# A float32 transformer layer on one core: the low half of the output weights made in three operations with a signal each

## What is computed

```
x = x + cross_attention(layernorm(x), ctx)     # 512 context tokens of width 384 for each batch
h = layernorm(x)
q, k, v = h @ wq, h @ wk, h @ wv               # self-attention within a batch of 64 tokens
q, k = rope(q), rope(k)
p = softmax(where(causal, q @ k.T / sqrt(32), -inf))
x = x + (p @ v) @ wo                           # wo: 512 x 512
h = layernorm(x)
top, idx = top_k(h @ w_router, 32)             # half of the tokens of each batch
y = gelu(h[idx] @ W1 + b1) @ W2 + b2           # 512 -> 2048 -> 512
x = x + (h with sigmoid(top) * y added at idx)
```

## Time and profile before

| what | value |
| --- | --- |
| median of 3 runs | 1198.59 us (1198.58 to 1198.82) |
| the profiled execution | 1198.52 us |
| its span, first to last instruction | 1196.7 us |
| PE busy | 1182.8 us, 99% of the span |
| DVE busy | 747.8 us, 62% |
| ACT busy | 624.0 us, 52% |
| POOL busy | 600.0 us, 50% |
| granted TensorE clock | 1.000 |

### The profile page before, as it was taken

One profiled execution on the slowest core, in us unless ns is written; L12 is line 12 of the kernel. 1 busy time (PEld: TensorE's weight loads), 2 busy tenths in 40 slices (PEclk: granted clock), 3 DMA queues, 4 the chain that ended last, 5 costly groups with the idle time before them and its releaser, 6 DMA issues.

```text
span 1196.7 us, 32636 instructions
## 1 busy us (share of the span) xinstructions
PE 1182.8 (99%) x12300; PEld 943.2 (79%) x12300; DVE 747.8 (62%) x1833; ACT 624.0 (52%) x1232; POOL 600.0 (50%) x331
## 2 busy tenths in 40 slices
PE   7999999999999999999999999999999999999998
PEld 6877777777777777777777777798888888888886
DVE  4256657657656756756666665558887899527223
ACT  6456556656656656656656566752222437434431
POOL 6932352432532532532523528557666664665663
PEclk9999999999999999999999999999999999999999
DMA  8044555555555555555555453110110013343431
GB/s 292 30 139 134 152 138 133 150 137 140 138 140 140 136 138 150 126 139 149 126 140 154 126 133 107 56 61 19 24 24 20 20 38 107 124 139 115 161 122 62
DMA packets 89314, 137.01 MB, mean 114 GB/s; under 512 B 20768, under 2 KB 25120, under 8 KB 89248
## 3 DMA queue, kind: packets, MB, share of 16 engines
q1 hardware_dynamic: 82208, 124.01, 36.9%
q10 hardware_dynamic: 5760, 7.87, 2.8%
q0 software_dynamic: 1280, 4.20, 1.0%
HBM read 63.39 MB, written 6.29 MB: 58 GB/s over the span
## 4 chain that ended last, share of the span: by engine, by line
PE 92%; SPq 3%; DVE 2%; issue 1%; POOL 1%; ACT 1%; DMA 1%; POOLq 0%; DVEq 0%
PE psum L220 42%; PE psum L1145 7%; PE psum L1883 7%; PE psum L2223 7%; PE psum L249 5%; PE psum L238 5%; PE psum L294 4%; PE psum L1173 3%; PE psum L1134 3%; PE psum L883 3%; SPq L558 2%; PE psum L1186 1%; PE psum L1229 1%; PE psum L280 1%; PE psum L1166 1%
## 5 line engine op out<-in xcount | busy, mean ns | idle before, releaser
L418 DVE CUSTOM_DVE_ANT_0 prob<-psum,mbias 128x512 f32<-128x512 f32 x256 | 165.4, 684 | 201.8 <-PE psum L238 193.7
L336 ACT ACTIVATE prob<-prob,nmx 128x512 f32<-128x512 f32 x256 | 182.6, 714 | 102.1 <-DVE nmx L418 71.0
L342 ACT ACTIVATE prob<-prob,rinv 128x512 f32<-128x512 f32 x256 | 176.3, 711 | 0.0
L604 POOL TENSOR_SCALAR ctx_a<-ctx_r 128x1536 fp32r<-128x1536 f32 x16 | 65.5, 4095 | 218.9 <-DMA ctx_r<-in_ctx 199.8
L441 DVE STREAM_TRANSPOSE blocks<-prob 128x512 f32<-128x512 f32 x240 | 162.9, 698 | 12.0 <-ACT prob L342 12.0
L367 ACT ACTIVATE V<-psum 128x512 f32<-128x512 f32 x120 | 71.7, 598 | 166.2 <-PE psum L220 166.2
L604 POOL TENSOR_SCALAR ctx_b<-ctx_r 128x1536 fp32r<-128x1536 f32 x16 | 65.5, 4092 | 183.8 <-PE psum L220 161.0
L220 PE MATMUL psum<-ctx_b,wk_h 128*128 128x512 f32 x384 | 127.2, 398 | 0.0
L220 PE MATMUL psum<-ctx_a,wk_h 128*128 128x512 f32 x384 | 126.8, 398 | 0.0
L220 PE MATMUL psum<-wv_h,ctx_b 128*128 128x512 f32 x384 | 124.7, 391 | 0.0
L220 PE MATMUL psum<-wv_h,ctx_a 128*128 128x512 f32 x384 | 124.0, 390 | 0.0
(11 more groups left out here) (256 smaller groups left out, 2833.7 us busy)
## 6 DMA issues: line engine op xcount, KB each, us to landing
turned<-blocks SPq DMA_DIRECT2D x840, 64.0 KB
ctx_r<-in_ctx SPq DMA_DIRECT2D x32, 768.0 KB
w_r<-in_L_ffn_W SPq DMA_DIRECT2D x64, 256.0 KB, 2.9
turned<-blocks ACTq DMA_DIRECT2D x120, 64.0 KB
xres<-in_x SPq DMA_DIRECT2D x16, 256.0 KB
out<-tok SPq DMA_DIRECT2D x16, 256.0 KB, 2.0
pX<-squares SPq DMA_DIRECT2D x52, 64.0 KB, 2.0
tok<-in_x SPq DMA_DIRECT2D x3, 1024.0 KB, 12.0
```

The source lines that it names most:

```text
L336: act.activation(prob[:, r, :], prob[:, r, :], ACT.Exp, bias=nmx[:, r:r + 1], scale=-1.0, accum_out=rsum[:, r:r + 1]).then_inc(s_ex, 1)
L342: act.activation(prob[:, r, :], prob[:, r, :], ACT.Copy, scale=rinv[:, r:r + 1]).then_inc(s_pn, 1)
L418: dve.tensor_tensor_reduce(prob[:, r, :], S_bank[r], mbias[:, b, :], 1.0, 3.0e38, ALU.add, ALU.min, nmx[:, r:r + 1]).then_inc(s_mx, 1)
L604: pool.tensor_scalar(y[:, 0], ctx_r[:], 1.0, None, ALU.mult).then_inc(s_cx, 1)
```

## The change

VectorE makes `ow_l` by three operations instead of one, for parts 0, 1 and 2 to 3 of the four, and each adds one to `s3_wd`. In step 2 TensorE waits for one, two, three and three signals ahead of the four parts of the output projection, and its wait for `s3_od` stands ahead of those. ScalarE's later wait asks for three signals instead of one. The new lines shift the line numbers of the changed kernel: by 4 behind L1310, by 9 behind L1533, by 11 behind L1546.

```diff
@@ pe3
             if has(t - 2):
                 pe.wait_ge(s3_rq, min(2 * t + 6, 2 * G) if isinstance(t, int) else 2 * t + 6)
+                pe.wait_ge(s3_od, t - 1)
                 if isinstance(t, int) and t == 2:
-                    pe.wait_ge(s3_wd, 1)
-                pe.wait_ge(s3_od, t - 1)
-                output_projection(pe, par).then_inc(s3_Wo, 1)
+                    for n in range(DT):
+                        pe.wait_ge(s3_wd, min(n + 1, 3))
+                        ins = output_projection(pe, par, parts=(n,))
+                    ins.then_inc(s3_Wo, 1)
+                else:
+                    output_projection(pe, par).then_inc(s3_Wo, 1)
@@ act3
             if isinstance(t, int) and t == G - 5:
-                act.wait_ge(s3_wd, 1)
+                act.wait_ge(s3_wd, 3)
@@ before dve3
+        def dve_low_output(dve, parts):
+
+            dve.tensor_tensor(ow_l[:, parts], ow_r[:, parts], ow_h[:, parts].bitcast(F32),
+                              ALU.subtract).then_inc(s3_wd, 1)
@@ dve3
                 dve.wait_ge(s3_wa, 1)
-                dve.tensor_tensor(ow_l[:], ow_r[:], ow_h[:].bitcast(F32), ALU.subtract).then_inc(s3_wd, 1)
+                dve_low_output(dve, slice(0, 1))
+                dve_low_output(dve, slice(1, 2))
+                dve_low_output(dve, slice(2, DT))
```

## The result

| | before | changed |
| --- | --- | --- |
| median of 19 runs | 1198.64 us (1197.15 to 1199.36) | 1200.80 us (1199.75 to 1202.68) |
| ratio, 95% interval | | 1.002 (1.0014 to 1.0026) |
| the profiled execution | 1198.52 us | 1201.28 us |
| its span | 1196.7 us | 1199.5 us |
| third step, scores to scores | 14.42 us | 16.71 us |

The kernel became slower by 0.2%, some 2.4 us (1.7 to 3.1). The ratio gives that; the medians differ by 2.16. The forecast was 1200.9 us, 2.31 us more than before. The last two rows of the table go by the start of the scores (L1186) on TensorE's timeline: 824.33 and 838.75 us before, 824.86 and 841.57 now. The third step alone is longer, by 2.29 us, and nothing behind it has changed. The 0.53 us by which the step began later in this one execution belong to what lies ahead of it, which differs from one execution to the next.

What follows compares the result with a forecast made beforehand. TensorE bounds the kernel, and in the third step VectorE's `r_sin` decides when it goes on. 1198.52 us plus 2.31 is 1200.83; the median lies 0.07 above, so 1200.9 us, range 1198.6 to 1201.5.

Steps and rivals of the forecast that it cites:

- What bounds: TensorE, and in the third step VectorE's queue behind `ao_l`: Third step: VectorE's end of `r_sin` decides when TensorE goes on; at most 0.81 us could be won.
- Three more waits on TensorE cost nothing: Output projection: the added TensorE waits fall into time in which it waits anyway; cost nothing.
- Three operations cost little by themselves: VectorE's `ao_l`: without company three operations cost a little more than one, ending 0.17 us late.
- GpSimd gets a turn at each of the two boundaries: Between the `ao_l` pieces: GpSimd's `r_sin`, then `qT`, get in; VectorE is 2.31 us late.
- The handovers: Between VectorE and GpSimd around the pieces: the next operation really starts 0.15 us before the other's recorded end.
- An estimate from that figure: Two handovers to GpSimd, by the Trainium skill's 115 ns: 0.265 us later each, 1201.4 us in all.
- TensorE's idle time: Third step: TensorE waits 1.2 us inside the output projection and 1.5 us before the values projection.
- The 1212 us: TensorE's clock falling to half for one step of 13.6 us; a small part of the slower rival's 0.07.
- with one turn: At the `ao_l` boundaries GpSimd gets in only once; 1.24 us late, 1199.8 us; chance 0.08.
- with none: VectorE keeps its turn through all `ao_l` pieces; 0.17 us late, 1198.8 us; chance 0.11.
- with a gain: L1134's wait has another cause than VectorE's `r_sin`, so the early start stays won; 1198.1 us; chance 0.03.
- the slower one: Each handover at the `ao_l` boundaries costs more, deciding from 0.02 us on each of four; 1201.5 us; chance 0.07.

Runs made afterwards that it cites:

- e3: The full change, but GpSimd waits for all three `ao_l` signals before its first rotation of the third step; ratio to before 1.0003.
- e7: Against the kernel before: GpSimd makes `ow_l` in two halves in its first and second step, VectorE's operation is gone; 1197.45 us, ratio 0.9996.
- e6: Against the kernel before: VectorE's single `ow_l` operation moved to the end of the second step; ratio 1.0002.
- e2: Against the kernel before: only TensorE's waits ahead of the four output projection parts, all for one signal, VectorE's operation left whole; ratio 0.9999.
- the second copy of before: The kernel before, run again without any edit; 1198.55 us median, third step 14.48 us, ratio 1.0001.
- e1: The full change without TensorE's separate waits: VectorE's three operations, and TensorE waits once for all three; ratio to before 1.0031.
- e5: The change with four VectorE pieces of 512 elements and four signals instead of three pieces; ratio to before 1.002.

## Why the prediction was right

*What bounds: TensorE, and in the third step VectorE's queue behind `ao_l`.* Right. e3 shows it alone: with the output projection free to start at once, TensorE still went on only behind `r_sin`. e7 shows the reverse: with the operation out of the queue both waits are gone, and 0.81 us are won, where a cause of L1134's own would have left at most 0.46. In e6 the expectation was right in the step and missed the place where the moved operation was paid for.

*Three more waits on TensorE cost nothing.* Right, e2: 0.01 us from the second copy of before.

*Three operations cost little by themselves.* Right, 0.17 us forecast, 0.14 measured in e3 (2.67 against 2.53).

*GpSimd gets a turn at each of the two boundaries.* Right, and it is where the time is. The forecast had the pieces at 0.9, 1.8 and 2.3 us and GpSimd's operations at 1.7 and 1.5; measured are 0.93, 1.76, 2.31, 1.72 and 1.50. The 0.19 us by which `qT` asked in time were enough, in all three kernels with three or more pieces and GpSimd free (the change, e1, e5). The handovers, forecast 0.15 us ahead of the recorded ends, come out at 0.17, 0.13, 0.14 and 0.14 from the rows above, with the undisturbed lengths that the forecast used.

The Trainium skill ("SBUF — State Buffer", "A bandwidth-pool intuition that's wrong") gives 115 ns behind the end for a transfer whose descriptors GpSimd writes, held up by a VectorE copy, and not for an operation of GpSimd like these. An estimate from that figure had the pieces end 0.5 us later, and the trace speaks against carrying it over. The rule of the Trainium skill ("SBUF — State Buffer", "Who interferes with whom") that the two engines exclude each other for whole instructions agrees with all of these rows.

*TensorE's idle time.* Forecast 1.2 and 1.5 us, measured 1.1 and 1.4 on the matmuls. Less the 0.53 us by which this execution reached the step later, the output projection began at 825.17 and the values projection at 831.00, where the forecast had 825.24 and 831.02. The granted clock stayed at 1.00. The 1212 us that the forecast set against a fall of the clock was added up wrongly: with the 2.31 us it would have been 1214.5.

*The total.* 2.31 us forecast, 2.29 in the step, 2.16 between the medians, 1.002 the ratio. That the first two agree within 0.02 us is partly luck, since two copies of one kernel differ by 0.06 in the step. The rivals with one turn, with none, and with a gain are excluded by the changed kernel's own rows; the slower one would have needed a step of 16.8 us or more. (Its 0.02 us on each of four handovers make 2.39, which does not yet pass 2.4; it needed a little more than that.) On which side of 0.2% the kernel lies is not settled by 19 runs (0.14% to 0.26%); the forecast had left that open too.

## What to carry to other kernels

Before you cut an operation in pieces so that its consumer can start sooner, ask two things of the trace: what the consumer waits for next, and who is held up by the operation as long as it is whole. Here the next wait hung on the same queue, so an early start could win nothing; and each boundary let a waiting engine in for a whole instruction, at a price close to that instruction's length (1.15 and 1.17 us for instructions of 1.30), where the boundary alone cost 0.08. If the operation has to be off the queue, look for a pause into which it fits whole, with what follows it in view: e7 found one on the other engine, e6 did not in the step before.

## What the runs showed that was not expected

The same three operations took 4.85 us or 2.67, only by whether GpSimd had been told to wait, and GpSimd's own operation ended 0.5 us later for it than beside the one operation. Here a semaphore kept GpSimd out of a run of VectorE operations with two SBUF inputs, at almost no price, since GpSimd would have been held up anyway.

In e7 an edit at 800 to 814 us lengthened a place at 1017 us by 0.3 us, in both of its runs, through the same two engines' turns: VectorE's CAST, which has a single SBUF input, took 2.58 us behind GpSimd's `w_l`, against 2.29 in the kernel before at the same place, and 0.43 where no operation of GpSimd lay beside it (at 1013.08 and 1013.98 us). So it is not only VectorE operations with two SBUF inputs that GpSimd's can hold up.
